# Feed-forward slots of 512, 512, 512, 256, 256 rows and a last block of 128 rows in unsplit float32

## The reference

```python
x = x + 0.5 * ffn(layernorm(x)); x = x + attn(layernorm(x)); x = x + 0.5 * ffn(layernorm(x))
```

```python
probs = softmax(x @ w_router.T); top = argmax(probs); weight = probs[top]
h = einsum('nd,ehd->enh', x, w_fc)            # 512 -> 2048, for each expert
a = square(where(h >= 0, h, 0.5 * h))
out = sum over e of (a @ w_proj[e].T) * (top == e) * weight
```

## Time and profile before

| | us |
|---|---|
| median of 3 runs (2169.43 to 2173.05) | 2172.9 |
| the profiled execution | 2155.2 |
| its span, first to last instruction | 2153.6 |
| PE busy in it | 2015.6 |

### The profile page before, as it was taken

One profiled execution on the slowest core, in us unless ns is written; L12 is line 12 of the kernel. 1 busy time (PEld: TensorE's weight loads), 2 busy tenths in 40 slices (PEclk: granted clock), 3 DMA queues, 4 the chain that ended last, 5 costly groups with the idle time before them and its releaser, 6 DMA issues. The chain is left out here.

```text
span 2153.6 us, 30604 instructions
## 1 busy us (share of the span) xinstructions
PE 2015.6 (94%) x11728; PEld 1657.9 (77%) x11728; DVE 1400.0 (65%) x2607; ACT 669.4 (31%) x1156; POOL 284.5 (13%) x244
## 2 busy tenths in 40 slices
PE   2999999959999999999999999999999499999996
PEld 2788888857887878878878878878887378888875
DVE  5775666767666665666666666666667567566666
ACT  3444444534121222212221221212222144344443
POOL 3100001031020020110110110201202103000013
PEclk9999999989999999999999999999999699999998
DMA  5342333430010010000100100100101135432346
GB/s 214 139 145 97 128 104 136 158 121 13 1 38 9 7 31 8 18 28 1 37 9 1 37 9 1 37 9 8 30 1 40 55 143 111 143 128 96 127 134 228
DMA packets 46943, 149.75 MB, mean 70 GB/s; under 512 B 5856, under 2 KB 5856, under 8 KB 46816
## 3 DMA queue, kind: packets, MB, share of 16 engines
q1 hardware_dynamic: 38544, 121.13, 17.2%
q0 software_dynamic: 8272, 26.76, 3.6%
HBM read 125.83 MB, written 22.04 MB: 69 GB/s over the span
## 5 line engine op out<-in xcount | busy, mean ns | idle before, releaser
L1249 PE MATMUL at_pj<-at_w_lo,at_xT_hi 128*128 128x512 f32 x512 | 209.9, 410 | 0.0
L1249 PE MATMUL at_pj<-at_w_hi,at_xT_lo 128*128 128x512 f32 x512 | 200.8, 392 | 0.0
L1249 PE MATMUL at_pj<-at_w_hi,at_xT_hi 128*128 128x512 f32 x512 | 200.7, 392 | 0.0
L1223 PE MATMUL at_pj<-at_xT_hi,at_w_lo 128*128 128x512 f32 x384 | 158.5, 413 | 11.5 <-issue 10.5
L583 DVE TENSOR_TENSOR last_ff_w_lo<-last_ff_stage,last_ff_w_hi 128x1024 fp32r<-128x1024 f32 x80 | 98.0, 1225 | 97.7 <-ACT last_ff_w_hi L416 97.7
L583 DVE TENSOR_TENSOR first_ff_w_lo<-first_ff_stage,first_ff_w_hi 128x1024 fp32r<-128x1024 f32 x80 | 98.0, 1225 | 89.6 <-ACT first_ff_w_hi L416 89.5
L1223 PE MATMUL at_pj<-at_xT_hi,at_w_hi 128*128 128x512 f32 x384 | 151.5, 395 | 0.0
L1223 PE MATMUL at_pj<-at_xT_lo,at_w_hi 128*128 128x512 f32 x384 | 151.5, 394 | 0.0
L866 POOL TENSOR_TENSOR at_coef<-at_ms,minus_half 128x4 f32<-128x4 f32 x64 | 63.5, 1009 | 559.0 <-DVE at_ms L1181 559.0
L842 POOL TENSOR_TENSOR at_w_lo<-at_stage,at_w_hi 128x1024 fp32r<-128x1024 f32 (+1 forms) x36 | 78.5, 2181 | 392.4 <-ACT at_w_hi L906 392.4
L1203 DVE TENSOR_TENSOR xres<-at_r,xres 128x512 f32<-128x512 f32 x128 | 88.2, 689 | 62.2 <-PE at_r L1403 62.2
(11 more groups left out here) (308 smaller groups left out, 4768.0 us busy)
## 6 DMA issues: line engine op xcount, KB each, us to landing
first_ff_stage<-wff SPq DMA_DIRECT2D x80, 512.0 KB, 3.5
last_ff_stage<-wff SPq DMA_DIRECT2D x80, 512.0 KB, 3.5
at_stage<-watt SPq DMA_DIRECT2D x24, 512.0 KB, 3.6
at_stage<-watt SPq DMA_DIRECT2D x16, 384.0 KB, 3.2
xres<-x SPq DMA_DIRECT2D x4, 1024.0 KB, 9.9
first_ff_xg<-sorted_rows SPq DMA_DIRECT2D x4, 1024.0 KB, 6.1
slot_rows<-first_ff_y POOLq DMA_DIRECT2D x4, 1024.0 KB, 6.5
last_ff_xg<-sorted_rows SPq DMA_DIRECT2D x4, 1024.0 KB, 7.2
```

The lines of the kernel that those rows point to most:

```text
L1223: last = pe.matmul(PJ[(7 * k + part) % 2][:, :], wq(w, kk, part), x[:, kk, tok], start=(kk == 0 and n == 0), stop=(kk == KC - 1 and n == 2))
L1249: last = pe.matmul(PJ[(7 * k + 3 + t) % 2][:, :], x[:, kk, tok], wvg(w, kk), start=(kk == 0 and n == 0), stop=(kk == KC - 1 and n == 2))
```

## The change

There are now six slots: three of 512 rows, two of 256 and an edge block of 128. The first five cover each row once; the edge block covers the 128 rows with the border a second time, for the other expert. The slots are written out; there is no loop. `late_slots` is rewritten for the new table, with about as many small DVE instructions as before, and `weights` reads the new entries.

In the edge block nothing is split. PE multiplies plain float32: `up_edge` reads the weights from `stage` and the turned rows from `xe` (a view of `xg`), 4 matmuls of 128 columns; `down_edge` reads `edge_a(t)` and `stage`, one matmul of 512 columns. ACT only squares, DVE makes factor and product. A `stage` buffer of the edge block is loaded again after `down_done` instead of after the splits. In the second feed-forward `behind_by` is 5: rows are added from step 5 on, one a step, and two in each of the last five. The late gather, add and scatter cover one tile of 128 rows instead of two.

```diff
-SLOTS = GROUPS + 1
-BLOCK = GROUP // 2
-BLOCKS = TOK // BLOCK
+WIDTHS = (GROUP, GROUP, GROUP, GROUP // 2, GROUP // 2, P)
+SLOTS = len(WIDTHS)
+EDGE = SLOTS - 1
+BLOCK = P
+BLOCKS = 2 * GROUP // BLOCK
...
+        xe = xg[:, GT - 1, :].rearrange("p (k t) -> p k t", k=KC)
...
-        KNOWN = GROUPS + 1
+        KNOWN = 3
+        act_copied = [sum((w // P + 1) // 2 for w in WIDTHS[:j]) for j in range(SLOTS + 1)]
+        dve_copied = [sum(w // P // 2 for w in WIDTHS[:j]) for j in range(SLOTS + 1)]
...
-        takes_piece = lambda j, t: x_in is not None and isinstance(j, int) and j == GROUPS - 1 and t % piece_step == 0
+        takes_piece = lambda j, t: x_in is not None and j == EDGE - 3 and t % piece_step == 0
...
+        def edge_a(t):
+            return a[:, t % 2, (t // 2 % 2) * P:(t // 2 % 2 + 1) * P]
+
         def all_slots(engine, slot_body):
 
-            slot_body(0, GROUP, GROUP)
-            with engine.Fori(1, GROUPS - 1) as j:
-                slot_body(j, GROUP, GROUP)
-            slot_body(GROUPS - 1, GROUP, BLOCK)
-            slot_body(GROUPS, BLOCK, 0)
+            for j in range(SLOTS):
+                slot_body(j, WIDTHS[j], WIDTHS[j + 1] if j < EDGE else 0)
...
                     if after or t < HT:
-                        sp.wait_ge(w_hi_done, j * HT + t + 1)
-                        sp.wait_ge(w_lo_done, j * HT + t + 1)
+                        if j < EDGE:
+                            sp.wait_ge(w_hi_done, j * HT + t + 1)
+                            sp.wait_ge(w_lo_done, j * HT + t + 1)
+                        else:
+                            sp.wait_ge(down_done, j * HT + t + 1)
                         load_w(tile0 if t < HT else tile0_next, t)
...
-                pool.wait_ge(y_act, j * 2 + width // P // 2 + 1)
-                pool.wait_ge(y_dve, j * 2 + width // P // 2 + 1)
+                pool.wait_ge(y_act, act_copied[j + 1] + 1)
+                pool.wait_ge(y_dve, dve_copied[j + 1] + 1)
...
-                    act.activation(xT_hi[:, k, 0:width], ps_x[k % 2][:, 0:width], ACT.Copy).then_inc(x_hi_done, 1)
+                    act.activation(xT_hi[:, k, 0:width] if j < EDGE else xe[:, k, :], ps_x[k % 2][:, 0:width], ACT.Copy).then_inc(x_hi_done, 1)
...
+                    if t == 0 and j < EDGE:
                         split_w(j, AHEAD)
                     act.wait_ge(up_done, j * HT + t + 1)
+                    if j == EDGE and t >= 2:
+                        act.wait_ge(a_done, j * HT + t - 1)
                     act.activation(square[:, t % 2, 0:width], ps_h[t % 2][:, 0:width], ACT.Square).then_inc(square_done, 1)
+                    if j == EDGE:
+                        continue
...
+                    if j + 1 < EDGE and t + AHEAD >= HT:
...
@@ -539,34 +549,35 @@
             def late_slots():
...
+                dve.tensor_reduce(border[:, 2:3], blocks[:, 0:BLOCKS:2], op=ALU.add, axis=AX.X)
+                dve.scalar_tensor_tensor(out=table[:, 1, 2:3], in0=table[:, 0, 2:3], scalar=float(GROUP), in1=rest_rows[:, 1:2], op0=ALU.mult, op1=ALU.add)
+                step(dve.tensor_scalar(reach[:, 0:1], table[:, 0, 2:3], -float(GROUP), float(GROUP), ALU.mult, ALU.add))
+                dve.tensor_tensor(reach[:, 1:2], border[:, 0:1], reach[:, 0:1], ALU.subtract)
+                dve.tensor_tensor(table[:, 1, 3:4], rest_rows[:, 1:2], reach[:, 0:1], ALU.add)
...
-            behind_by = 3
+            behind_by = 5
...
-                    if t == 0:
+                    if t == 0 and j < EDGE:
...
+                    if j == EDGE and t >= RING:
+                        dve.wait_ge(down_done, j * HT + t + 1)
+                    dve.tensor_tensor(edge_a(t) if j == EDGE else a[:, t % 2, 0:width],
+                                      square[:, t % 2, 0:width], factor[:, t % 2, 0:width], ALU.mult).then_inc(a_done, 1)
...
+                    if j == EDGE:
+                        continue
...
+                    if j + 1 < EDGE and t == HT - 1:
...
+                if j + 1 < EDGE:
...
+                    if j == EDGE:
+                        pe.wait_ge(x_hi_done, j * KC + k - 1)
+                    elif not first or k >= 2:
                         pe.wait_ge(x_lo_done, j * KC + k - 1)
...
+                def up_edge(t):
+                    r = t % RING
+                    pe.wait_ge(w_loaded[r], (j * (HT // RING) + t // RING + 1) * 16)
+                    pe.wait_ge(square_done, j * HT + t + 1)
+                    pe.wait_ge(factor_done, j * HT + t + 1)
+                    for k in range(KC):
+                        if t == 0:
+                            pe.wait_ge(x_hi_done, j * KC + k + 1)
+                        last = pe.matmul(ps_h[t % 2][:, 0:P], stage[:, r, k * P:(k + 1) * P], xe[:, k, :], start=(k == 0), stop=(k == KC - 1))
+                    last.then_inc(up_done, 1)
+
+                def down_edge(t):
+                    pe.wait_ge(a_done, j * HT + t + 1)
+                    if t == 0:
+                        pe.wait_ge(y_act, act_copied[j] + 1)
+                    pe.matmul(ps_y[0][:, :], edge_a(t), stage[:, t % RING, D:2 * D], start=(t == 0), stop=(t == HT - 1)).then_inc(down_done, 1)
+
...
                             last = pe.matmul(ps_y[i][:, :], x[:, r, i * P:(i + 1) * P], w[:, r, D:2 * D],
                                              start=(t == 0 and n == 0), stop=(t == HT - 1 and n == 2))
                     last.then_inc(down_done, 1)
+                if j == EDGE:
+                    for t in range(HT + AHEAD):
+                        if t < HT:
+                            up_edge(t)
```

More of the change, by code:

```diff
@@ L148, in phase_feed_forward @@
         mv, vare, nmean, rstd, shift = (norms[n] for n in ("mv", "vare", "nmean", "rstd", "shift"))
-        gap, is1, cum, zero, tok, rest, behind, pos, row_i, slot = (r[n] for n in (
-            "gap", "is1", "cum", "zero", "tok", "rest", "behind", "pos", "row_i", "slot"))
+        gap, is1, cum, zero, tok, rest, behind, pos, row_i, edges = (r[n] for n in (
+            "gap", "is1", "cum", "zero", "tok", "rest", "behind", "pos", "row_i", "edges"))
         mag = sb("rt_mag", [P, TILES])
@@ L442, in slot_body @@
                     act.activation(a_hi[:, t % RING, 0:width], a[:, t % 2, 0:width], ACT.Copy).then_inc(a_hi_done, 1)
-                    if after and t + AHEAD >= HT:
+                    if j + 1 < EDGE and t + AHEAD >= HT:
                         split_w(j, t + AHEAD)
@@ L545, in late_slots @@
-                dve.tensor_scalar(rest_rows[:, 3:4], rest_rows[:, 0:1], -float(GROUP), float(3 * GROUP), ALU.mult, ALU.add)
-                dve.tensor_scalar(blocks[:], slot[:], float(BLOCK), border[:, 0:1], ALU.mult, ALU.is_lt)
-                step(dve.tensor_scalar(table[:, 1, 0:GROUPS], slot[:, 0:GROUPS], float(GROUP), float(BLOCK), ALU.mult, ALU.add))
-                dve.tensor_copy(slot_table[:, 1, 2:GROUPS], rest_rows[:, 2:4])
-                dve.tensor_scalar(rest_rows[:, 2:4], rest_rows[:, 2:4], float(BLOCK), border[:, 0:1], ALU.add, ALU.is_ge)
@@ new lines, in late_slots @@
+                step(dve.tensor_scalar(reach[:, 0:1], table[:, 0, 2:3], -float(GROUP), float(GROUP), ALU.mult, ALU.add))
+                dve.tensor_tensor(reach[:, 1:2], border[:, 0:1], reach[:, 0:1], ALU.subtract)
+                dve.tensor_tensor(table[:, 1, 3:4], rest_rows[:, 1:2], reach[:, 0:1], ALU.add)
+                step(dve.scalar_tensor_tensor(out=table[:, 0, EDGE:SLOTS], in0=border[:, 2:3], scalar=2.0, in1=border[:, 1:2], op0=ALU.mult, op1=ALU.subtract))
+                dve.tensor_scalar(table[:, 0, 3:4], reach[:, 1:2], float(P), None, ALU.is_lt)
@@ new lines, in late_slots @@
+                dve.tensor_scalar(table[:, 0, 4:5], reach[:, 1:2], float(3 * P), None, ALU.is_lt)
+                dve.tensor_scalar(table[:, 1, 4:5], table[:, 1, 3:4], float(GROUP // 2), None, ALU.add)
+                step(dve.scalar_tensor_tensor(out=border[:, 3:4], in0=border[:, 1:2], scalar=float(P), in1=rest_rows[:, 1:2], op0=ALU.mult, op1=ALU.add))
+                step(dve.tensor_scalar(table[:, 1, EDGE:SLOTS], border[:, 3:4], float(TOK - P), None, ALU.min))
+                dve.tensor_copy(slot_table[:, 1, 2:SLOTS], table[:, 1, 2:SLOTS])
@@ L562, in weights @@
+                dve.tensor_scalar(slot_table[:, 0, 2:SLOTS], table[:, 0, 2:SLOTS], float(HT), None, ALU.mult).then_inc(table_ready, KNOWN - 2)
             def weights():
-                step(dve.tensor_scalar(behind[:], pos[:], table[:, 1, GROUPS:SLOTS], None, ALU.subtract))
+                step(dve.tensor_scalar(behind[:], pos[:], table[:, 1, EDGE:SLOTS], None, ALU.subtract))
                 step(dve.tensor_scalar(inside[:], behind[:], 0.0, None, ALU.is_ge))
                 step(dve.scalar_tensor_tensor(out=inside[:], in0=behind[:], scalar=float(BLOCK), in1=inside[:], op0=ALU.is_lt, op1=ALU.mult))
-                step(dve.scalar_tensor_tensor(out=inside[:], in0=is1[:], scalar=border[:, 5:6], in1=inside[:], op0=ALU.is_equal, op1=ALU.mult))
```

(3 more changed lines are left out.)

67 lines of the change are left out of this document (28 added, 39 removed).

## The result

| | median us | lowest to highest | ratio to before, 95% interval |
|---|---|---|---|
| before | 2173.05 (7 runs) | 2169.43 to 2175.46 | |
| changed kernel | 2179.81 (7 runs) | 2177.71 to 2183.31 | 1.0034 [1.0025, 1.0043] |

The change makes the kernel 7.4 us slower (0.0034 of 2173; 5.4 to 9.3 by the interval). The forecast was 2177, in a range of 2160 to 2198, with "slower" the likeliest sign. The time came out close, but by luck: large errors of opposite sign met in the sum, as the stages show.

The account below looks back on a forecast made before the run. PE, busy 94% of the span, was read as the bound, with the edge block waiting on weight loads. First feed-forward +4.8 and second -0.95 summed to +3.9, about 4 us: 2177 us beside the median, range 2160 to 2198.

Parts of the forecast that it names:

- slower: Whole kernel: the change makes it slower than before, chance 0.42 against 0.31 for faster and 0.27 for same.
- Step 1: One 512-row slot becomes two of 256, with one PE stall of 1.0 us: +4.8 us per feed-forward.
- Step 2: First feed-forward's last block: steps wait for weight loads gated by down(t-4); -0.3 us, plus 1.2 for queued second loads.
- the rival of a PE-bound block: Edge block: loads are hidden and steps take 1.83 us, 31 instead of 47.7 us; 2144 us in all, chance 0.05.
- The landing: Edge block's weight loads: time to landing taken as 4.3 us in the first feed-forward, 4.6 in the last.
- the term for a second load that queues: Edge block: a pair's second load may queue behind the first's data; 0.2 us a pair, +1.2 per feed-forward.
- the rival of fast landing: Edge block: weight loads may land in 3.4 us as in wide slots; -13 us, 2164 us in all, chance 0.16.
- Step 3: End of the first feed-forward: one y tile stored instead of two before the attention's gathers; -0.9 us (0 to -1.1).
- Step 4: Second feed-forward's end: last row -4.9 us, queued loads +1.2, burst of `out` stores +0.5, one late tile -2.55.
- The clock rival: Edge block: PE's gaps of about 2.7 us each halve the clock for 3.2 us; +19, 2196 us, chance 0.18.

Follow-up runs that it names:

- Experiment 4: The changed kernel without the split: four slots of 512 rows and the edge block of 128; 2170.27 us, ratio 0.9983.
- experiment 2: The changed kernel with eight weight buffers instead of four in the last block, so a load waits for down(t-8); 2149.62 us, ratio 0.9885.
- experiment 8: The changed kernel with all 16 residual additions of the second feed-forward's last block made behind its last step; 2188.48 us, ratio 1.0076.
- experiment 3: The changed kernel with the stores of `out` issued by ScalarE, one step behind each added row, instead of on SP; 2182.15 us, ratio 1.0036.
- experiment 9: The changed kernel with the first seven `out` stores issued between the last block's last seven weight loads; 2168.72 us beside 2163.28 for before, ratio 1.0030.

## Why the prediction came out near, step by step

| step | forecast | measured in the traces |
|---|---|---|
| 1. split, each feed-forward | +4.8 | +6.3 and +6.1 |
| 2. first block | -0.3 + 1.2 | -3.8 (42.79 for 46.57, to the start of the last down record) |
| 3. end of the first feed-forward | -0.9 | -0.05 (21.14 for 21.19 us to the attention's first matmul) |
| first feed-forward | +4.8 | +2.5 |
| 4. second block and tail | -5.75 | +0.5 (70.46 for 69.93) |
| second feed-forward | -0.95 | +6.6 |
| sum | +3.9 | +9.1; by the ratio +7.4 (5.4 to 9.3) |

The sum of the steps lies in the interval of the measured ratio. It leaves out the stall and the attention, which vary in both kernels. The forecast of 2177 beside 2179.8 is luck: the first block was put 4.7 us too high, the split 2.8 too low over both feed-forwards, step 3 0.85 too low and the second block with its tail 6.3 too low.

**Step 1, the split: right mechanism, size 1.5 us short.** A step takes 2.82 us as forecast (328.92, 331.74, 334.56 are starts of ups in the first new slot), and the stall of 1.00 is there at both new transitions (1.00 and 0.79). But it doesn't cost only its own length. In the first new slot the three ups around it take 5.54 us in place of 3 x 1.42 and the next two groups 1.79 and 1.53 in place of 1.39 and 1.42: 1.8 us in all, and 1.6 in the next. The trace of before has the same 5.54 and 1.79 in its 256-row slot; I took the bracket of the earlier trace rows for the whole price. Experiment 4 puts the split at 11 us of the kernel's time, and at 9.0 in its trace, since the block behind a narrower slot is quicker.

**Step 2, the first block: right mechanism, one term wrong.** The waits are on `stage` loads, and experiment 2 takes them away and with them 15 us, which is the rival of a PE-bound block made true. Its forecast of 31 us counts the last two downs twice, since 16 x 1.83 = 29.3 holds them already; to the same point, the end of the last down, 28.2 was measured (27.72 + 0.43), and 43.2 for the changed kernel's block where 47.7 was forecast. The landing was the error: five pairs took 5.76 us each and not 6.73, 4.9 us in all. Of that 0.8 a pair is the landing, 3.5 us and not 4.3, and 0.2 is the term for a second load that queues: PE did wait 0.4 to 0.7 us for the second load, but the pair was no longer for it. What follows those pairs took some 0.5 us more than forecast. Two loads in 5.7 us are the same mean spacing as the 2.82 us of the rows that I relied on, so the spacing does not set the landing, as I had read the earlier trace rows; what does wasn't tried. It was the rival of fast landing, and it came true in the first feed-forward alone. Its reason, that every engine but PE is idle there, was a misreading: VectorE is busy for 10.0 us and ScalarE for 5.0 of the 42.8. The float32 down matmul was sized right: two records, 0.86 to 0.88 us in the chain for the 0.87 forecast.

**Step 3** gave 0.05 us and not 0.9. The smaller store did bring the gathers forward, 7.28 us behind the last down matmul and not 8.27, as forecast. But the first gathered row was added 12.59 us behind that matmul and 12.31 before: the first gather took about 5.3 us instead of 4.0. Why is not known.

**Step 4, the second block: wrong, and the largest error.** It was forecast that DVE leaves the path and the last row comes 4.9 us sooner; it came 2.0 sooner (51.1 us into the block for 53.1). With the gathers and additions taken out the block is as short as the first (experiment 8), so what I left out is that the gathers share the DMA engines with the loads on which the block now hangs: a load in the chain takes 5.86 us, the clock halves behind the wait, and a step's end slips. Of the 8.0 us by which the second block is longer than the first 3.7 are idle time of PE and 4.3 are more busy time (34.91 for 30.66 us), at the lower clock. From the last row to its store's landing it was 7.52 us (2162.33 to 2169.85) for 2.04 before: the burst costs 3.7 us of it and the slower landing the rest, where 0.5 was forecast with a bound of 1.5. The forecast counted ten issues in the burst; it was all 16, since the last load is issued at 2154.04 and no store comes before it. Behind it the single late tile saves 14.8 - 11.8 = 3.0 us, close to the 2.55 forecast. Experiments 3 and 9 show that the burst can be taken away, and that the block then takes back part or all of it; only in experiment 2, which removes the gate, is the block short (33.79) and the last store issued as soon as its row is added; its tail is 18.51 all the same, since the last row comes late from a gather. That the burst and the block trade with each other is shown by the traces; how much of the time it is worth is not.

**The clock rival** had its place right and its size wrong. In the first block gaps up to 2.79 us left the clock at 1.00. In the second, behind the gap of 2.89 us, the next eight records still took 1.16 us, but the two of down after them 1.78 in place of 1.02 and the eight after those 1.91 in place of 1.05; behind the gap of 3.43 us eight records took 2.08. These stretches ran at a granted clock of 0.51 and 0.50, that is 1.2 GHz; over the whole block it is 0.90. The length of one gap does not tell which way it goes: in the second block of experiment 4 a gap of 2.47 us had 2.08 us for eight records behind it, and in that of experiment 9 a gap of 3.26 had 1.16 and a clock of 1.00 over the next 3.8 us. The Trainium skill (TensorE: Matmul & The Clock Gate, "HAM oscillation — how this bites in real kernels") warns of thin matmul bursts between waits for DMA: the second block agrees, with two falls in sixteen steps. The waits of the page's example, about 3 to 5 us, are longer than any of the first block, so the first block doesn't speak against it. Experiment 8 thins out the transfers, no wait exceeds 2.63 us and the clock stays at 1.00: the clock follows from the late loads, and it makes about half of their price.

**Open.** Why the engine's update of `x_turned` comes 5 to 12 us late while its matmuls run on. Of the nine profiles with the marks at that transition seven show it and two (the first of before, experiment 9) don't; of the two with the marks moved none does. That the small indirect stores bring it about is likely, since moving them gained 6 and 7 us with intervals that don't overlap in the first case and barely in the second; by what path isn't known. Nor is it known why the attention varies between 1235 and 1243 us.

## What to carry to other kernels

When a cheaper form of a step reads its input straight from the buffer that a load fills, count what the buffer's release now waits for: here the saved 15 us of TensorE became waits for loads that were issued too late, and four more buffers gave them back. Price such a load from both ends, and again where other transfers run beside it: the same block was 8 us longer there. And take a second profile of the kernel before subtracting two: 28 us lay between two single executions, 7 between the medians.

## What the runs showed of the hardware

- A float32 matmul of 512 columns shows as two records of 0.43 us spacing (0.86 to 0.88 us for two in the chain); the trace of before had only the 128-column one.
- A 512 KB weight load landed after 3.5 us in the median of the first block (two loads in 5.7 us) and 4.3 in the 256-row slot before (one in 2.82). It took up to 5.9 beside gathers of 256 KB (changed kernel), 5.9 beside a store of 1 MB (experiment 4), and up to 6.9 beside gathers and stores (experiment 3).
- The 16 stores issued on SP in a burst followed each other after 0.5 to 1.5 us, 0.77 in the mean (2154.41 to 2166.01), while a single weight load's issue took 0.33.
- Sixteen indirect stores of 1 KB each across a transition went, in seven of nine profiles, with a semaphore update that reached ScalarE 5.2 to 13.0 us after TensorE's transposes began, where 0.6 and 1.0 us are usual; moved, they went with gaps of 1.5 and 3.0 us elsewhere.
- TensorE's clock fell behind waits of 2.5 us (experiment 4) and stayed at its upper level behind one of 3.3 (experiment 9), in the same last block.
